# Three early steps of a two-layer float32 kernel: recurrence vector and W_out, Hadamard products in the T banks, norm factors

## The chip, the cores and the metric

The kernel runs on one core of one Trainium2 chip. The metric is the device time of one execution in microseconds (us), as a median of several runs. Engines are named as in the profile: PE is TensorE (matmuls; PEld its weight loads), DVE is VectorE, ACT is ScalarE, POOL is GpSimd, SP is SyncE, which here issues nearly all DMAs.

## What is computed

Input x is 4 x 512 x 256 in float32. Two layers, each: a layer norm, a token mixer s, a gated feed-forward g with its own three weights, and x + s * silu(g).

```
xn = layernorm(x)
# layer 0: the mixer is a recurrence whose state starts at zero, so only one step is left
xi  = xn @ W_in.T
y   = sum over states of (C_real * B_real - C_imag * B_imag) * xi      # (the theta terms multiply a zero state)
s   = xn + rmsnorm(y @ W_out.T, norm_w)
# both feed-forwards
hidden = fwht(silu(xn @ W1.T) * (xn @ W3.T)) ;  g = hidden @ W2.T       # fwht: Walsh-Hadamard over 1024
x = x + s * silu(g)
# layer 1: the mixer is causal attention with qkv, o_proj, gamma, beta, plus the residual
```

The Hadamard transform is moved from the activations to W2. The recurrence is folded into one 256 x 256 matrix M = W_in.T diag(k) W_out.T, with the vector k = sum over states of (B_real C_real - B_imag C_imag), and attention's weights into two matrices A and V.

## The kernel before

**Arithmetic.** Most products are float32 made of three TensorE passes: each operand is split into a high part (written by ACT, a copy to the type fp32r) and a low part (the difference, by DVE or POOL). `mm3` (L357 to L359) issues hi x hi, hi x lo, lo x hi. The products that make M, A and V (L425, L435, L440) are plain float32.

**Stages.** The tokens are four groups of 512 rows, and each layer passes over all four: eight groups n = 0 to 7. A group has eight chunks (0 to 7) of 128 hidden units: PE makes gate and up products into GU (`up_chunk`), ACT takes silu into `hf` (L721) and makes the high part of the last chunk's hidden (L647), DVE multiplies (L997, the `chunk` helper) and makes the low part (L841, `hid_lo_chunk`). Then PE mixes (`recurrent_mix` with M, or attention), and the next group begins with the down products of the last one (`down_chunk`, bank pair O).

**The head (group 0)** also has all preparation in it: turning and splitting W1, W3, W2, the Hadamard products and butterflies of W2 (butterflies on POOL, L1204 to L1218), and M, A, V. Every engine's order is written out by hand in its own `block0_head`. The steps around the change:

- DVE `k_vector` (L868 to L875) makes k; it waits for `small_loaded`, which nine loads raise: A_theta, B and C parts, W_in, norm_w, gamma, beta. It stands after chunk 4 and the next group's normalise (L914).
- ACT scales W_in's four parts by k (L759) after chunk 5.
- DVE `turn_wout` (L925, two transposes of `woutT`) stands after chunk 5.
- PE `small_m` (L425, 16 matmuls in the trace) stands after chunk 6 and waits for both of them; after chunk 7 comes `small_av` (L435, L440; it waits for DVE's `turn_wqkv`), then `recurrent_mix(0)`, and then PE waits for `sm_lo` at 3: DVE's low parts of M, A and V (`small_lo`).
- DVE's `w2_sums` (L857) and `w2_lo` and ACT's `w2_hi` (L688) finish W2 between chunks 6 and 7.

**The second layer's weights** are prepared in groups 1 to 3. For each of four pairs of W2 row blocks, PE makes a Hadamard product of two matmuls (`next_hadamard`, L401 and L402) into bank O[:, 1], and ACT scales it into U (`pair_u`, L670). The O bank is also what `down_chunk` writes, so groups 1 to 3 begin with a wait for `u_ready`, and `next_hadamard` waits for `gateT_ready` (ACT has read O). T's two banks are used in the head and in the attention scores and not between.

**The norm factors** of the second layer: POOL makes c2, DVE turns it into `c2T` (L976, `turn_c2`), SP stores it (L289) and spreads it to all partitions as `c2B` (L291). SP's queue is in order: in group 3 it holds the gate's transfer, then `spread_c2(0)`, then `move_rows(4)` (store `swap_rows`, L254, and four reads, L259). The rows that `move_rows` brings are scaled with c2B on DVE (L986), split on ACT (L702, L798, L647) and POOL (L1306), and PE's first attention product of group 4 (GU<-ZT,AR) needs them.

Of the kernel before, what the change touches and what calls it, by code (L numbers as in the profile page):

```python
# [22 lines left out]
ACT = mybir.ActivationFunctionType  # L23
AX_X = mybir.AxisListType.X

P = 128
# [6 lines left out]
def two_block_kernel(nc, x_in, W_in, W_out, A_theta, B_real, B_imag, C_real, C_imag, norm_w,  # L33
                     W1_0, W2_0, W3_0, qkv, o_proj, gamma, beta, W1_1, W2_1, W3_1, consts, out):
    NB, ROWS, D = x_in.shape
    H = W1_0.shape[0]
# [4 lines left out]
    MC = NM // P  # L41
    PAIRS = HC // 2
# [18 lines left out]
    with ExitStack() as ctx:  # L61
# [3 lines left out]
        def sem(name):  # L65
            return ctx.enter_context(nc.semaphore(name))
# [45 lines left out]
        with ExitStack() as early:  # L112
            win = sb("win", [P, MC, D], F32, early)
# [71 lines left out]
        c2_line = nc.dram_tensor("c2_line", [P, Q], F32).ap()  # L185
        c2_turned = sem("c2_turned")
        w_turned, wx_hi, wx_lo, natx_hi, natx_ready = sem("w_turned"), sem("wx_hi"), sem("wx_lo"), sem("natx_hi"), sem("natx_ready")
        wout_loaded, wqkv_loaded, wo_loaded = sem("wout_loaded"), sem("wqkv_loaded"), sem("wo_loaded")
        wout_turned, wqkv_turned, win_scaled = sem("wout_turned"), sem("wqkv_turned"), sem("win_scaled")
        xnext_loaded = sem("xnext_loaded")  # L190
# [34 lines left out]
        def _(sp):  # L225
# [74 lines left out]
            sp.wait_ge(w2_tr, 1)  # L300
            load_pair(0, 2, stage[:, 0, :, :], stage_loaded[0])
            for i, m in enumerate((A_theta, B_real, B_imag, C_real, C_imag)):
                sp.dma_start(ssm[:, i, :, :], m.rearrange("c (a p) s -> p (c a) s", p=P)).then_inc(small_loaded, 16)
            sp.dma_start(win[:, :, :], W_in.rearrange("(a p) k -> p a k", p=P)).then_inc(small_loaded, 16)
            load_blocks(woutT[:, :, :].rearrange("p m d -> p (m d)"), W_out, wout_loaded)
            sp.wait_ge(w2_tr, 2)
            load_pair(0, 3, stage[:, 1, :, :], stage_loaded[1])
# [39 lines left out]
                t_at = (NB - 1) * TILES  # L347
                sp.dma_start(last_part(out_dram, t_at, q), last_part(X, t_at, q)).then_inc(out_stored, 16)
            sp.wait_ge(out_stored, 16 * (NB - 1 + len(LAST_PARTS)))
        N_SMALL = 9  # L350


        @block.tensor
        def _(pe):
# [41 lines left out]

            def next_hadamard(i):

                pe.wait_ge(u_ready, i)
                pe.wait_ge(natx_ready, i - PAIRS + 1)  # L400
                pe.matmul(O[:, 1, :], hadmR[:, :], w2nat[:, 0, :, :].rearrange("p a d -> p (a d)"), start=True, stop=False)  # L401
                pe.matmul(O[:, 1, :], hadmR[:, :], w2nat[:, 1, :, :].rearrange("p a d -> p (a d)"), start=False, stop=True).then_inc(h_done, 1)  # L402

            def head_hadamard(i):
                if i == 0:
# [149 lines left out]
                pe.wait_ge(sm_lo, 3)  # L555

            def block0_group(n):
                pe.wait_ge(u_ready, PAIRS + (0, 1, 3)[n - 1])
                for i in range(HC):
                    down_chunk(0, n - 1, i)  # L560
                for c in range(HC):
                    up_chunk(0, n, c, False)
                    if c == 1 and n > 1:
                        pe.wait_ge(gateT_ready, 2 * n)
                        next_hadamard(PAIRS + 2 * n - 3)
                if n < 3:
                    pe.wait_ge(gateT_ready, 2 * n)
                    next_hadamard(PAIRS + 2 * n - 2)
                recurrent_mix(n)

# [73 lines left out]
        def _(act):  # L644
# [22 lines left out]
            def pair_u(l, i, j):  # L667

                act.wait_ge(h_done, i + 1)
                act.activation(U[l][:, 2 * j:2 * j + 2, :].rearrange("p a d -> p (a d)"), O[:, 1, :], ACT.Copy, scale=float(H) ** -0.5).then_inc(u_ready, 1)  # L670

            def nat_hi(i, nat):

                if not (isinstance(i, int) and i == 0):
                    act.wait_ge(h_done, i)
                hi(nat[:, 0, :, :].rearrange("p a d -> p (a d)"), O[:, 0, :], w2_tr, i + 1, w2nat_hi)
# [54 lines left out]
            def block0_head():  # L731
                act.dma_start(ident[:, :], consts[:, 0, :]).then_inc(ident_loaded, 16)
                flat = [R[:, 0, :, :].rearrange("p k d -> p (k d)") for R in (MR, AR, VR)]
                hi(W1T[0][:, 0, :, 0:2 * P], GU[:, 0, 0, :].rearrange("p (k h) -> p k h", k=KC), w_tr, 1, w_hi)
                first_x_hi()
                hi(W3T[0][:, 0, :, 0:2 * P], GU[:, 0, 1, :].rearrange("p (k h) -> p k h", k=KC), w_tr, 2, w_hi)
                nat_hi(0, w2nat)
                act.wait_ge(hadm_loaded, 16)
                act.activation(hadmR[:, :], hadm[:, :], ACT.Copy).then_inc(hadm_ready, 1)
                chunk(0, 0, True)  # L740
                pair_hi(0, 1, 1)
                pair_u(0, 0, 0)
                nat_hi(1, w2nat)
                chunk(0, 1, True)
                pair_u(0, 1, 1)
                pair_hi(0, 2, 2)
                nat_hi(2, w2nat)
                chunk(0, 2, True)
                chunk(0, 3, True)
                pair_u(0, 2, 2)  # L750
                pair_hi(0, 3, 3)
                nat_hi(3, w2nat)
                chunk(0, 4, True)
                chunk(0, 5, True)
                pair_u(0, 3, 3)
                hi(gb[:, :, :].rearrange("p g k -> p (g k)"), O[:, 0, 0:2 * KC], gb_tr, 1, gb_ready)
                act.wait_ge(kvec_ready, 1)
                for m in range(MC):
                    act.activation(win[:, m, :], win[:, m, :], ACT.Identity, scale=kvec[:, m:m + 1]).then_inc(win_scaled, 1)  # L759
                chunk(0, 6, True)  # L760
                hi(flat[0], O[:, 0, :], sm_mm, 1, sm_hi)
                w2_hi(0)
                chunk(0, 7, True)
                hid_hi_chunk(0, 7)
                small_hi([(flat[1], T[:, 0, :]), (flat[2], T[:, 1, :])], 2, sm_mm, 2, sm_hi)
                act.wait_ge(mask_loaded, 16)
                act.activation(identR[:, :], ident[:, :], ACT.Copy).then_inc(const_ready, 1)
                act.activation(maskR[:, :], mask[:, :], ACT.Copy).then_inc(const_ready, 1)
# [68 lines left out]
        def _(dve):  # L837
# [24 lines left out]

            def k_vector():

                dve.wait_ge(small_loaded, 16 * N_SMALL)
                flat = [ssm[:, i, :, :].rearrange("p a s -> p (a s)") for i in range(5)]
                kp = [kprod[:, i, :, :].rearrange("p a s -> p (a s)") for i in (0, 1)]
                dve.tensor_tensor(kp[0], flat[1], flat[3], ALU.mult).then_inc(kstep, 1)  # L868
# [148 lines left out]
            def between_chunks(n, c, last=False):  # L1017
# [12 lines left out]
                if c == 0 and not last:  # L1030
                    stats(n + 1, ((n + 1) % NB) * TILES)
                if c == (4 if n < NB else 3) and not last:
                    if n >= NB - 1:
                        turn_c2(n + 1)
                    dve.wait_ge(combined, 4 * n)
                    normalise(n + 1, ((n + 1) % NB) * TILES)
                if c == (5 if n < NB else 4) and not last:
                    x_turn(n + 1)
                if c == 5 and n >= NB:
                    p_lo(n - NB)  # L1040

# [27 lines left out]
            def block0_head():  # L1069
# [13 lines left out]
                pair_lo(0, 2, 2)  # L1083
                nat_lo(2, w2nat)
                chunk(0, 2)
                chunk(0, 3)
                dve.wait_ge(xnext_loaded, 16)
                pair_lo(0, 3, 3)
# [1 line left out]
                stats(1, TILES)  # L1090
                chunk(0, 4)
                normalise(1, TILES)
                k_vector()
                chunk(0, 5)
                turn_wout()
                x_turn(1)
                chunk(0, 6)
                turn_wqkv()
# [3 lines left out]
                chunk(0, 7)  # L1102
                w2_lo(0, 1)
                dve.wait_ge(xrest_loaded, 16)
                small_lo(1)
                small_lo(2)
                hid_lo_chunk(0, HC - 1)
# [245 lines left out]
```

## Time and profile before

| | us |
|---|---|
| median of 3 runs (362.18 to 363.77) | 362.24 |
| the profiled execution, its own time | 364.02 |
| its span, from first to last instruction | 362.2 |
| PE busy in the span | 353.7 (98%) |
| DVE busy | 251.1 (69%) |
| ACT busy | 167.7 (46%) |
| POOL busy | 104.2 (29%) |

The granted TensorE clock is full in all slices but one: 38 to 41.4 us is at half speed. PE's busy time counts matmuls with modelled ends, so it hides short gaps; start-to-start times of neighbouring matmuls show them better. A timeline row gives start, duration, engine, line, operation and operands, how many merged, and in brackets the idle time before it with what ended it.

### The profile page before, as it was taken

The numbers are of one execution on the slowest core, as the hardware profiler recorded it, in microseconds if no ns is written. First come the engines' busy times: TensorE is split into PE (matmuls) and PEld (weight loads), VectorE is DVE, ScalarE is ACT, GpSimd is POOL, SyncE is SP. The second block draws the span as 40 slices with busy tenths as digits, with TensorE's granted clock in tenths as the row PEclk, the third lists the DMA queues.
The fourth block names the chain that finished last, engine by engine and source line by source line (L and its number), as shares of the span: only waits on it lengthen the run. The fifth ranks groups of instructions, "written<-read, shape, count | busy, mean of one in ns | idle before, by whom it ended". The sixth has DMA issues, their size and how long they took to land.

```text
span 362.2 us, 4969 instructions
## 1 busy us (share of the span) xinstructions
PE 353.7 (98%) x1785; PEld 299.6 (83%) x1785; DVE 251.1 (69%) x482; ACT 167.7 (46%) x326; POOL 104.2 (29%) x122
## 2 busy tenths in 40 slices
PE   8998899999999999999999999999999999999996
PEld 5886788888888888887888888888888888888896
DVE  5669954896479945977568894688636887356645
ACT  2865361357135624345285544644446454454510
POOL 2165310165315953474007030060300603004000
PEclk9999899999999999999999999999999999999999
DMA  7999686305252303040142501424105342054001
GB/s 238 251 183 225 154 111 57 116 2 139 36 138 39 116 2 116 3 133 14 60 144 64 144 0 58 139 67 149 57 22 168 74 123 81 0 186 112 22 3 58
DMA packets 69648, 34.44 MB, mean 95 GB/s; under 512 B 40692, under 2 KB 69624, under 8 KB 69624
## 3 DMA queue, kind: packets, MB, share of 16 engines
q1 hardware_dynamic: 69480, 34.06, 37.0%
q8 instruction: 14, 0.23, 0.3%
q14 instruction: 10, 0.08, 0.1%
q10 hardware_dynamic: 144, 0.07, 0.1%
HBM read 21.99 MB, written 12.12 MB: 94 GB/s over the span
## 4 chain that ended last, share of the span: by engine, by line
PE 76%; DVE 12%; ACT 4%; DMA 3%; issue 2%; SPq 1%; POOL 1%; ACTq 0%; DVEq 0%
PE GU L357 14%; PE GU L359 14%; PE GU L358 14%; PE O L357 8%; PE O L358 7%; PE O L359 7%; DVE hid L841 3%; DVE hf L997 2%; DVE rows L1015 2%; PE O L425 1%; DMA stage<-in_L_ffn_W 1%; DVE rows L914 1%; DMA swap_rows<-GX 1%; PE T L357 1%; PE T L359 1%
## 5 line engine op out<-in xcount | busy, mean ns | idle before, releaser
L721 ACT ACTIVATE hf<-GU 128x512 f32<-128x512 f32 x64 | 38.2, 598 | 80.9 <-DVE hid L841 62.7
L997 DVE TENSOR_TENSOR hf<-hf,GU 128x512 f32<-128x512 f32 x64 | 43.5, 680 | 30.9 <-PE GU L359 25.0
L841 DVE TENSOR_TENSOR hid<-hf,hid 128x512 fp32r<-128x512 f32 x64 | 52.4, 820 | 0.3
L357 PE MATMUL GU<-XT,W1T 128*128 128x512 f32 x128 | 50.5, 395 | 0.0
L359 PE MATMUL GU<-XT,W1T 128*128 128x512 f32 x128 | 49.9, 390 | 0.0
L358 PE MATMUL GU<-XT,W1T 128*128 128x512 f32 x128 | 49.8, 389 | 0.0
L357 PE MATMUL GU<-XT,W3T 128*128 128x512 f32 x128 | 49.8, 389 | 0.0
L359 PE MATMUL GU<-XT,W3T 128*128 128x512 f32 x128 | 49.8, 389 | 0.0
L358 PE MATMUL GU<-XT,W3T 128*128 128x512 f32 x128 | 49.8, 389 | 0.0
L357 PE MATMUL O<-hid,W2hi 128*128 128x512 f32 x112 | 44.1, 394 | 0.7 <-ACT U L670 0.7
L358 PE MATMUL O<-hid,W2hi 128*128 128x512 f32 x112 | 43.7, 390 | 0.0
L359 PE MATMUL O<-hid,W2lo 128*128 128x512 f32 x112 | 43.7, 390 | 0.0
L647 ACT ACTIVATE hid<-hf 128x512 fp32r<-128x512 f32 x64 | 40.0, 624 | 6.2 <-DVE hf L997 6.2
L1265 POOL TENSOR_TENSOR X<-X,rows 128x256 f32<-128x256 f32 x28 | 24.3, 900 | 31.5 <-DVE rows L1015 31.5
L1223 POOL TENSOR_TENSOR vtmp<-varb,ln_eps 128x4 f32<-128x4 f32 x7 | 1.4, 201 | 98.2 <-DVE varb L909 98.2
L359 PEld LDWEIGHTS GU<-XT,W1T 128*128 128x128 f32 x128 | 24.0, 188 | 5.1
L359 PEld LDWEIGHTS GU<-XT,W3T 128*128 128x128 f32 x128 | 24.0, 188 | 5.1
L357 PEld LDWEIGHTS GU<-XT,W3T 128*128 128x128 f32 x128 | 24.0, 188 | 5.0
L358 PEld LDWEIGHTS GU<-XT,W3T 128*128 128x128 f32 x128 | 24.0, 188 | 5.0
L357 PEld LDWEIGHTS GU<-XT,W1T 128*128 128x128 f32 x128 | 24.0, 188 | 4.9 <-DVE hf L997 0.3
L358 PEld LDWEIGHTS GU<-XT,W1T 128*128 128x128 f32 x128 | 24.1, 188 | 4.6
L357 PEld LDWEIGHTS O<-hid,W2hi 128*128 128x128 f32 x112 | 21.0, 188 | 5.8 <-ACT U L670 1.1
(204 smaller groups left out, 724.4 us busy)
## 6 DMA issues: line engine op xcount, KB each, us to landing
swap_rows<-GX SPq DMA_DIRECT2D x7, 512.0 KB, 3.4
sT<-swap_rows SPq DMA_DIRECT2D x28, 128.0 KB, 2.7
swap_gate<-GX SPq DMA_DIRECT2D x7, 512.0 KB, 2.9
sT<-swap_gate SPq DMA_DIRECT2D x28, 128.0 KB, 2.8
stage<-in_L_ffn_W SPq DMA_DIRECT2D x12, 256.0 KB, 4.5
swap_p<-PX SPq DMA_DIRECT2D x4, 640.0 KB, 3.2
PL<-swap_p SPq DMA_DIRECT2D x16, 160.0 KB, 3.2
stage<-in_L_ffn_W SPq DMA_DIRECT2D x32, 64.0 KB, 2.7
```

Of the source, the lines that this page charges most:

```text
L357: pe.matmul(o, lhs(0), rhs(0), start=start, stop=False)
L358: pe.matmul(o, lhs(0), rhs(1), start=False, stop=False)
L359: return pe.matmul(o, lhs(1), rhs(0), start=False, stop=stop)
L425: last = pe.matmul(O[:, 0, k * D:(k + 1) * D], win[:, m, k * P:(k + 1) * P], woutT[:, m, :], start=(m == 0), stop=(m == MC - 1))
L647: act.activation(dst, src, ACT.Copy).then_inc(done, 1)
L721: act.activation(hf[:, c % 2, :], GU[:, c % 2, 0, :], ACT.Silu).then_inc(silu_done, 1)
L841: dve.tensor_tensor(dst, src, hi_part.bitcast(F32), ALU.subtract).then_inc(done, 1)
L914: last = dve.tensor_scalar(rows2[n % 2][:, t, :], X[:, bass.ds(x_at + t, 1), :].rearrange("p a d -> p (a d)"), mv[:, t, 0:1], rstd[:, t:t ...
L997: dve.tensor_tensor(hf[:, c % 2, :], hf[:, c % 2, :], GU[:, c % 2, 1, :], ALU.mult).then_inc(mul_done, 1)
L1015: dve.tensor_tensor(st, st, turned[:, :, t, :, :].rearrange("p j k a -> p k j a"), ALU.mult).then_inc(prod_ready, 1)
L1223: pool.tensor_tensor(vtmp[:, :], varb[:, :], ln_eps[:, :], ALU.add).then_inc(rstd_step, 1)
L1265: pool.tensor_tensor(xt, xt, rows2[n % 2][:, t, :], ALU.add).then_inc(combined, 1)
```

## The change

1. **Recurrence's vector.** The six loads of k and W_in get a semaphore of their own, `kv_loaded`; `small_loaded` keeps three. `k_vector` moves on DVE from after `normalise(1)` to after chunk 2, and ACT's scaling of W_in from after chunk 5 to before chunk 4. The order of the loads stays.
2. **W_out's turn** moves on DVE from after chunk 5 to before it.
3. **Hadamard products** of the second layer are written to T[:, i % 2] and read from there; the waits for `gateT_ready` go, the wait for `u_ready` becomes one lower, and only group 1 still begins with a wait for `u_ready`.
4. **Norm factors.** In group 3 alone, `turn_c2` moves from before `normalise` at chunk 4 to the end of chunk 3.

```diff
-                sp.dma_start(ssm[:, i, :, :], m.rearrange("c (a p) s -> p (c a) s", p=P)).then_inc(small_loaded, 16)
-            sp.dma_start(win[:, :, :], W_in.rearrange("(a p) k -> p a k", p=P)).then_inc(small_loaded, 16)
+                sp.dma_start(ssm[:, i, :, :], m.rearrange("c (a p) s -> p (c a) s", p=P)).then_inc(kv_loaded, 16)
+            sp.dma_start(win[:, :, :], W_in.rearrange("(a p) k -> p a k", p=P)).then_inc(kv_loaded, 16)
...
             def next_hadamard(i):
 
-                pe.wait_ge(u_ready, i)
+                pe.wait_ge(u_ready, i - 1)
                 pe.wait_ge(natx_ready, i - PAIRS + 1)
-                pe.matmul(O[:, 1, :], hadmR[:, :], w2nat[:, 0, :, :].rearrange("p a d -> p (a d)"), start=True, stop=False)
-                pe.matmul(O[:, 1, :], hadmR[:, :], w2nat[:, 1, :, :].rearrange("p a d -> p (a d)"), start=False, stop=True).then_inc(h_done, 1)
+                pe.matmul(T[:, i % 2, :], hadmR[:, :], w2nat[:, 0, :, :].rearrange("p a d -> p (a d)"), start=True, stop=False)
+                pe.matmul(T[:, i % 2, :], hadmR[:, :], w2nat[:, 1, :, :].rearrange("p a d -> p (a d)"), start=False, stop=True).then_inc(h_done, 1)
...
             def block0_group(n):
-                pe.wait_ge(u_ready, PAIRS + (0, 1, 3)[n - 1])
+                if n == 1:
+                    pe.wait_ge(u_ready, PAIRS)
...
                     if c == 1 and n > 1:
-                        pe.wait_ge(gateT_ready, 2 * n)
                         next_hadamard(PAIRS + 2 * n - 3)
                 if n < 3:
-                    pe.wait_ge(gateT_ready, 2 * n)
                     next_hadamard(PAIRS + 2 * n - 2)
...
-                if c == (4 if n < NB else 3) and not last:
-                    if n >= NB - 1:
+                    if n >= NB:
                         turn_c2(n + 1)
...
+                if c == 3 and n == NB - 1:
+                    turn_c2(n + 1)
```

The two moves within DVE's head are best seen in its order of instructions. From after chunk 4's second half to x's turn, before (kprod and kvec are the recurrence's vector, hf<-hf,GU is a chunk's product, hid<-hf,hid the low part of the chunk before it, GX<-rows the turn of x):

```order
L914 TENSOR_SCALAR rows<-X,mv,rstd 128x256 x4
L868 TENSOR_TENSOR kprod<-ssm 128x64
L869 TENSOR_TENSOR kprod<-ssm 128x64
L871 SCALAR_TENSOR_TENSOR kprod<-ssm,kprod 128x64
L873 TENSOR_TENSOR kprod<-kprod 128x64
L875 TENSOR_REDUCE kvec<-kprod 128x4
L997 TENSOR_TENSOR hf<-hf,GU 128x512
L841 TENSOR_TENSOR hid<-hf,hid 128x512
L925 STREAM_TRANSPOSE woutT<-woutT 128x512 x2
L954 STREAM_TRANSPOSE GX<-rows 128x4x4x32 x2
L997 TENSOR_TENSOR hf<-hf,GU 128x512
L841 TENSOR_TENSOR hid<-hf,hid 128x512
```

The same place now (all line numbers are one higher):

```order
L998 TENSOR_TENSOR hf<-hf,GU 128x512
L842 TENSOR_TENSOR hid<-hf,hid 128x512
L915 TENSOR_SCALAR rows<-X,mv,rstd 128x256 x4
L926 STREAM_TRANSPOSE woutT<-woutT 128x512 x2
L998 TENSOR_TENSOR hf<-hf,GU 128x512
L842 TENSOR_TENSOR hid<-hf,hid 128x512
L955 STREAM_TRANSPOSE GX<-rows 128x4x4x32 x2
L998 TENSOR_TENSOR hf<-hf,GU 128x512
L842 TENSOR_TENSOR hid<-hf,hid 128x512
```

And after chunk 2's two instructions (the first two rows here), where chunk 3's product stood next:

```order
L998 TENSOR_TENSOR hf<-hf,GU 128x512
L842 TENSOR_TENSOR hid<-hf,hid 128x512
L869 TENSOR_TENSOR kprod<-ssm 128x64
L870 TENSOR_TENSOR kprod<-ssm 128x64
L872 SCALAR_TENSOR_TENSOR kprod<-ssm,kprod 128x64
L874 TENSOR_TENSOR kprod<-kprod 128x64
L876 TENSOR_REDUCE kvec<-kprod 128x4
L998 TENSOR_TENSOR hf<-hf,GU 128x512
```

Between the chunk's products and x's turn the five small instructions are gone, W_out's two transposes are ahead of chunk 5 and no longer behind it, and the five stand ahead of chunk 3.

On PE, the end of group 1 and the start of group 2: the last mixing product and the first down product. Before:

```order
L357 MATMUL GU<-MR,XT 128x256
L358 MATMUL GU<-MR,XT 128x256
L359 MATMUL GU<-MR,XT 128x256
L357 MATMUL O<-hid,W2hi 128x512 [waits w2_ready,hid_ready,u_ready]
L358 MATMUL O<-hid,W2hi 128x512
L359 MATMUL O<-hid,W2lo 128x512
```

Now:

```order
L358 MATMUL GU<-MR,XT 128x256
L359 MATMUL GU<-MR,XT 128x256
L360 MATMUL GU<-MR,XT 128x256
L358 MATMUL O<-hid,W2hi 128x512 [waits w2_ready,hid_ready]
L359 MATMUL O<-hid,W2hi 128x512
L360 MATMUL O<-hid,W2lo 128x512
```

The wait for `u_ready` at the first down product is gone. On DVE in group 3, from chunk 2's product to x's turn, before:

```order
L997 TENSOR_TENSOR hf<-hf,GU 128x512
L841 TENSOR_TENSOR hid<-hf,hid 128x512
L997 TENSOR_TENSOR hf<-hf,GU 128x512
L841 TENSOR_TENSOR hid<-hf,hid 128x512
L976 STREAM_TRANSPOSE c2T<-c 128x32
L914 TENSOR_SCALAR rows<-X,mv,rstd 128x256 x4
L997 TENSOR_TENSOR hf<-hf,GU 128x512
L841 TENSOR_TENSOR hid<-hf,hid 128x512
L954 STREAM_TRANSPOSE GX<-rows 128x4x4x32 x2
```

Now:

```order
L998 TENSOR_TENSOR hf<-hf,GU 128x512
L842 TENSOR_TENSOR hid<-hf,hid 128x512
L977 STREAM_TRANSPOSE c2T<-c 128x32
L998 TENSOR_TENSOR hf<-hf,GU 128x512
L842 TENSOR_TENSOR hid<-hf,hid 128x512
L915 TENSOR_SCALAR rows<-X,mv,rstd 128x256 x4
L998 TENSOR_TENSOR hf<-hf,GU 128x512
L842 TENSOR_TENSOR hid<-hf,hid 128x512
L955 STREAM_TRANSPOSE GX<-rows 128x4x4x32 x2
```

The turn of the norm factors (c2T<-c) stands one chunk earlier.

## Rows read from the trace of the kernel before

**Rows 1.** PE's waits: engine, tile, line, what ended them; total, times, longest (us)

```profile
PE O L425 <- issue: 2.4, 1, 2.4
PE O L357 <- ACT U L670: 0.7, 2, 0.4
```

**Rows 2.** Timeline, PE in the head

```profile
37.23 5.38 PE L425 MATMUL O<-woutT,win 128*128 128x256 f32 x16 [2.40 <-issue]
...
45.18 1.89 PE L435 MATMUL T<-wqkvT 128*128 128x256 f32 x8
...
51.51 0.39 PE L357 MATMUL O<-hid,W2hi 128*128 128x512 f32 x1
```

**Rows 3.** Stretch: sum; busy of PE, PEld, DVE, ACT, POOL; granted clock; DMA share; GB/s

```profile
38.00:39.00 1.00, 1.00 (x4) 0.82 (x3) 1.00 (x3) 0.00 (x0) 1.00 (x1) 0.50 0.62 96
```

**Rows 4.** Timeline, DVE in the head

```profile
24.13 0.69 DVE L997 TENSOR_TENSOR hf<-hf,GU 128x512 f32<-128x512 f32 x1 [1.43 <-PE GU L359]
...
32.23 0.22 DVE L868 TENSOR_TENSOR kprod<-ssm 128x64 f32<-128x64 f32 x1
...
33.57 0.68 DVE L997 TENSOR_TENSOR hf<-hf,GU 128x512 f32<-128x512 f32 x1
34.16 1.75 DVE L841 TENSOR_TENSOR hid<-hf,hid 128x512 fp32r<-128x512 f32 x1
35.84 1.29 DVE L925 STREAM_TRANSPOSE woutT<-woutT 128x512 f32<-128x512 f32 x2
37.06 1.25 DVE L954 STREAM_TRANSPOSE GX<-rows 128x512 f32<-128x512 f32 x2
...
38.81 1.21 DVE L841 TENSOR_TENSOR hid<-hf,hid 128x512 fp32r<-128x512 f32 x1
39.95 1.88 DVE L925 STREAM_TRANSPOSE wqkvT<-wqkvT 128x512 f32<-128x512 f32 x3
...
49.46 0.69 DVE L841 TENSOR_TENSOR VR<-T,VR 128x512 fp32r<-128x512 f32 x1 [0.79 <-ACT VR L647]
```

**Rows 5.** Timeline, POOL in the head

```profile
34.08 1.28 POOL L1211 TENSOR_TENSOR U<-U 128x512 f32<-128x512 f32 x1
...
37.12 2.36 POOL L1218 TENSOR_TENSOR U<-U 128x1024 f32<-128x1024 f32 x1
```

**Rows 6.** Timeline, ACT in the head

```profile
33.69 1.71 ACT L759 ACTIVATE win<-win,kvec 128x256 f32<-128x256 f32 x4 [1.21 <-DVE kvec L875]
```

**Rows 7.** Timeline of SP's queue: W_out's four loads

```profile
14.54 3.78 SPq L242 DMA_DIRECT2D woutT<-in_L_attn_W_out  x4
```

**Rows 8.** The tile woutT: landing time of its four loads after issue

```profile
DMA to landing us min/median/max: 4.5/5.0/5.2
```

**Rows 9.** Timeline, PE from group 1 to group 2

```profile
87.38 0.28 PE L359 MATMUL GU<-MR,XT 128*128 128x256 f32 x1
88.01 0.50 PE L357 MATMUL O<-hid,W2hi 128*128 128x512 f32 x1 [0.35 <-ACT U L670]
```

**Rows 10.** Timeline from group 3 to group 4: DVE, SP's queue, ACT, PE

```profile
151.83 0.20 DVE L976 STREAM_TRANSPOSE c2T<-c 128x32 f32<-128x32 f32 x1
...
154.14 0.38 SPq L291 DMA_DIRECT2D c2B<-c_line  x1
155.91 0.36 SPq L254 DMA_DIRECT2D swap_rows<-GX  x1
...
164.61 1.16 ACT L702 ACTIVATE XT<-sT 128x512 fp32r<-128x512 f32 x2 [1.03 <-DMA sT<-swap_rows]
...
169.92 0.50 PE L357 MATMUL GU<-ZT,AR 128*128 128x512 f32 x1 [0.43 <-POOL ZT L1306]
```

**Rows 11.** The chain of waits, in order of time, at the same place

```profile
155.91 4.47 DMA swap_rows<-GX
```

**Rows 12.** The tile swap_rows: landing time of its stores and reads

```profile
DMA to landing us min/median/max: 2.3/2.8/4.5
```

**Rows 13.** The tile c2B: landing time of its four loads

```profile
DMA to landing us min/median/max: 4.8/4.9/5.0
```

More of the change, by code:

```diff
@@ L187, in two_block_kernel @@
         w_turned, wx_hi, wx_lo, natx_hi, natx_ready = sem("w_turned"), sem("wx_hi"), sem("wx_lo"), sem("natx_hi"), sem("natx_ready")
+        kv_loaded = sem("kv_loaded")
         wout_loaded, wqkv_loaded, wo_loaded = sem("wout_loaded"), sem("wqkv_loaded"), sem("wo_loaded")
@@ L349, in _ @@
             sp.wait_ge(out_stored, 16 * (NB - 1 + len(LAST_PARTS)))
-        N_SMALL = 9
+        N_KV, N_SMALL = 6, 3
         @block.tensor
@@ L669, in pair_u @@
                 act.wait_ge(h_done, i + 1)
-                act.activation(U[l][:, 2 * j:2 * j + 2, :].rearrange("p a d -> p (a d)"), O[:, 1, :], ACT.Copy, scale=float(H) ** -0.5).then_inc(u_ready, 1)
+                bank = O[:, 1, :] if l == 0 else T[:, i % 2, :]
+                act.activation(U[l][:, 2 * j:2 * j + 2, :].rearrange("p a d -> p (a d)"), bank, ACT.Copy, scale=float(H) ** -0.5).then_inc(u_ready, 1)
             def nat_hi(i, nat):
@@ L752, in block0_head @@
                 nat_hi(3, w2nat)
+                act.wait_ge(kvec_ready, 1)
+                for m in range(MC):
+                    act.activation(win[:, m, :], win[:, m, :], ACT.Identity, scale=kvec[:, m:m + 1]).then_inc(win_scaled, 1)
                 chunk(0, 4, True)
@@ L756, in block0_head @@
                 hi(gb[:, :, :].rearrange("p g k -> p (g k)"), O[:, 0, 0:2 * KC], gb_tr, 1, gb_ready)
-                act.wait_ge(kvec_ready, 1)
-                for m in range(MC):
-                    act.activation(win[:, m, :], win[:, m, :], ACT.Identity, scale=kvec[:, m:m + 1]).then_inc(win_scaled, 1)
                 chunk(0, 6, True)
@@ L863, in k_vector @@
             def k_vector():
-                dve.wait_ge(small_loaded, 16 * N_SMALL)
+                dve.wait_ge(kv_loaded, 16 * N_KV)
                 flat = [ssm[:, i, :, :].rearrange("p a s -> p (a s)") for i in range(5)]
@@ L1085, in block0_head @@
                 chunk(0, 2)
+                k_vector()
                 chunk(0, 3)
@@ L1092, in block0_head @@
                 normalise(1, TILES)
-                k_vector()
+                turn_wout()
                 chunk(0, 5)
-                turn_wout()
                 x_turn(1)
@@ L1104, in block0_head @@
                 dve.wait_ge(xrest_loaded, 16)
+                dve.wait_ge(small_loaded, 16 * N_SMALL)
                 small_lo(1)
```

## Prediction

> **What bounds the kernel now.** TensorE does. I read the list of PE's waits first [rows 1]: outside the start it waits at three kinds of place only, and each is one that the change aims at, so the question is not whether PE's waits are the bound but how much of each wait is left when its present cause is gone. The first is 2.40 us ahead of `small_m`, marked "issue" because several semaphores end it. The timelines tell which [rows 2, 4, 6]: ACT ends the scaling of W_in at 33.69 + 1.71 = 35.40, DVE ends the turn of W_out at 35.84 + 1.29 = 37.13, and PE starts at 37.23. So W_out's turn is last and the scaled W_in stands only 1.7 us ahead of it; both must move for the wait to go. The wait has a second price. `small_m` takes 5.38 us for 16 matmuls, while eight of the same shape take 1.89 [rows 2]; two such eights would take 3.8, so it runs 1.6 us longer. The stretches say why: a little after PE's idle time the granted clock is 0.50, the 1.2 GHz level [rows 3]. The second kind are two waits on ACT's U at the start of groups 2 and 3, 0.7 us in all [rows 1, 9]. The third is 0.43 us on POOL's ZT at the start of group 4 [rows 10].
>
> **Part 1 and 2: the head.** *The vector.* Its five DVE instructions take 33.57 - 32.23 = 1.34 us [rows 4] and go into a slot in which DVE idled 1.43 us for PE, ahead of chunk 3's product at 24.13. So they cost nothing there, if their six loads have landed by about 22.7. The trace doesn't show W_in's landing. It was issued just ahead of W_out's four loads, of which the first began to issue at 14.54 and each landed 4.5 to 5.2 us after issue [rows 7, 8]; taken as the nearest row this gives about 19.7 for W_in, 3 us early. From the other side it had landed by 32.23, where the vector was made without a wait for it. I take 19.7 and keep 32.23 for a rival. *Scaling W_in*, 1.71 us on ACT [rows 6], now stands before chunk 4's silu, which becomes about 1 us later; DVE multiplies that chunk only after the next group's statistics, so it doesn't notice. Cost nothing. *W_out's turn*, 1.29 us, takes exactly the place that the vector leaves, and ends at about 33.45. `small_m` then has all inputs when chunk 6 is done, at 37.23 - 2.40 = 34.83.
>
> So far PE would gain 2.40 + 1.6 = 4.0 us. The question is who is late next. PE would reach `small_av` at about 41 (before: 45.18) and the end of the mixing at about 47.5 (before: 51.51). What it needs there is DVE's: first the turned qkv, then `sm_lo` at 3, the low part of V. DVE was full from 30.9 to 42.9, and the moves take 1.3 us out of that stretch. Do its later steps come 1.3 us earlier? The rows say mostly not. A low part `hid<-hf,hid` reads two SBUF tensors and takes about 0.7 us when POOL is quiet, but 1.75 at 34.16, where POOL's butterfly had begun at 34.08, and 1.21 at 38.81, inside POOL's 37.12 to 39.48 [rows 4, 5]: each ends some 0.5 us after a POOL instruction does. The transposes at 35.84 and 37.06 run at full rate beside the same POOL work. With W_out's turn gone from behind it, x's turn comes at 35.8, chunk 6's product at 37.0, and the low part after it asks at 37.6, where POOL's long butterfly has just begun. It waits until 39.4 and ends at 39.9, as before. The turn of qkv is then at 39.9, as before [rows 4], and the 1.3 us are lost to a wait. Everything behind it on DVE (w2_sums, the parts of W2, chunk 7) keeps its time but for 0.1 to 0.2 us, and of the row at 49.46 only the 0.79 us of waiting for ACT's V goes, since PE makes V earlier now. So V's low part is ready at 49.46 + 0.69 - 0.79 - 0.15 = 49.2, PE starts the down products there, and **the head gains 51.51 - 49.2 = 2.3 us**. Two short idle times of about 0.8 us are new on PE, ahead of `small_av` (41.0 to 41.8) and ahead of the down products (48.3 to 49.2).
>
> The upper bound is 4.0, all of PE's loss. It is reached if the low part that asked at 34.16 gets in ahead of POOL. This is close: it now asks at 32.23 + (37.06 - 35.84) + 0.59 = 34.04, and POOL asks at 34.08, or at 34.00 if its first butterfly is no longer slowed by the small products of the vector. The lower bound is 0.6: both new idle times bring the slow clock, at up to 1.6 each less what the wait for DVE hides; the nearest rows are 2.40 us of idle time, which brought it, and 0.43, which didn't.
>
> The Trainium skill says in "SBUF — State Buffer", section "Who interferes with whom", that a DVE instruction with two SBUF inputs and a GpSimd one contend for a shared port pair, held for a whole instruction by whichever issues first, and that a DVE instruction with one SBUF input doesn't contend. The trace agrees with it: 1.75 against 0.7 us, and the transposes undisturbed. It speaks against this change: if the engines shared evenly and nothing waited, the head would give its 4.0 us; by the rule it gives 2.3.
>
> **Part 3: the Hadamard products.** No instruction is added. From the last mixing product to the first down product PE takes 88.01 - 87.38 = 0.63 us where mixing products follow each other at 0.12, and the first one back takes 0.1 longer for its weights; so 0.6 us at each of two places [rows 9], though the wait list has 0.35 [rows 1]. With U's copy out of T, the next thing to be late would be chunk 7's low part, which the third down chunk needs 2.7 us later; it ends at 87.6. So **1.2 us**. Bounds 0.7 (the waits as listed) and 1.3. The dropped waits for gateT_ready ended nothing in the list of waits: 0. Nobody else uses T in these groups.
>
> **Part 4: the norm factors.** DVE's c2T comes at about 149.9 and not 151.83; its 0.20 us fall into an idle time ahead of chunk 4. c2B then is issued at about 152.1 instead of 154.14 [rows 10]. The store of the rows is still issued at about 155.8, since DVE's turn of x sets that. In the trace it took 4.47 us to land where the median of this tile is 2.8 [rows 11, 12], and c2B, 4.9 us to land [rows 13], was under way for 3.1 us of it. With 1.2 us left of that overlap I take 1.0 us earlier for the rows; bounds 0 (overlap isn't the cause) and 1.7. ACT has idled 1.03 us for them [rows 10], so at most that passes on. PE's wait of 0.43 with the refill behind it, 0.7 by start-to-start times as in part 3, needs 0.6 us. So **0.7 us**, bounds 0 and 0.7.
>
> **Sum.** 2.3 + 1.2 + 0.7 = 4.2 us. Everything behind group 4 is bound by PE without a wait, so it shifts whole. The profiled execution's 364.02 us, 1.8 outside its span, would be 359.8; the median of the runs is 362.24, 1.8 less, and I carry the difference over: **358.0 us**.
>
> **Rivals.** (A) *DVE wins the tie at 34.04.* Then chunk 4's low part is done at 34.7, POOL is set back 0.6 us, the turn of qkv comes at 37.7 and V's low part at about 47.1, before PE asks. No wait of PE is left in the head: 4.0 + 1.2 + 0.7 = 5.9, time 356.3. For it: 0.04 us on one side; against: POOL's first butterfly is probably 0.08 earlier too, and at 0.08 us POOL won in this trace. (B) *A smaller sum*: one new idle time brings the slow clock (1.6), or part 4 gives nothing (0.7) together with part 3's lower bound (0.5). Times 359.6 and 359.2; both new idle times slow, 361. (C) *Slower.* DVE takes its steps in order, so if the six loads land late, the wait for kv_loaded holds chunk 3's product, and with it PE's chunk 5, which starts at 28.4 and needs that product. With a landing at L, PE loses L + 0.9 + 0.7 - 28.4. It eats the 4.2 us from L = 31.0 on; at 32.2, the latest that the trace allows, it is 5.4 us lost, 363.4. Against it are the loads behind these ones, landed by 23. (D) *It doesn't do what it says*: another input ends `small_m`'s wait at about 37 and only parts 3 and 4 are left, 360.3.
>
> **Chances.** Forecast 0.58, A 0.25, B 0.10, C 0.02, D 0.05. A measurement of this kernel can tell 0.5%, 1.8 us, from no change: faster is below 360.4. The forecast, A, most of B and half of D lie there, 0.93; I say 0.92. Within it 0.06, slower 0.02. The range takes in A, with 0.4 for its own error, and B's single slow clock: 355.9 to 359.8, leaving out C, D and the worst of B.
>
> **What the profile after would show.** Head: no idle time ahead of `small_m`, which takes 3.6 us at full clock; PE idle ahead of L436 and of the first down product at the head's end, 0.8 each; DVE's low part after chunk 6 long, some 2.3 us, and qkv's turn at 39.9 (in rival A at 37.7, and the idle times gone). At the starts of groups 2 and 3 no wait on U. In group 3 swap_rows landing in about 3.4 us and no wait on ZT. I am wrong if DVE waits for kv_loaded at 22.7, if the low part behind chunk 5 is 0.7 us long, or if PE's clock falls at a new idle time.

## The result, and the profile after

The changed kernel takes 357.88 us (median of 5 runs, 357.71 to 358.28). The kernel before, run beside it, takes 362.18 us (5 runs). The ratio is 0.987, with a 95% interval of 0.9848 to 0.9893, so the change gains 4.3 us. The prediction was 358.0. The number held, but the head did not go as forecast: two errors there nearly cancel, and most of what follows is about how they do.

PE's waits in the changed kernel, all of them (engine, tile, line, what ended them; total, times, longest, in us). In the rows of after, PE's and most of DVE's lines stand one number higher than in [rows 1 to 10], POOL's four higher:

```profile
PE GU L526 <- DVE hf L1073: 1.5, 1, 1.5
PE GU L365 <- DMA stage<-in_L_ffn_W: 0.4, 1, 0.4
PE GU L365 <- DVE rows L899: 0.3, 1, 0.3
```

All three lie in the first 9 us. Every wait of [rows 1, 10] is gone. The table of engines can't show this: PE is at 98% of a span of 356.1 us, as it was before:

```profile
PE   350.6 (98%) x1785; PEld 297.9 (84%) x1785; DVE 248.8 (70%) x482; ACT 167.5 (47%) x326; POOL 105.2 (30%) x122
```

The head after, as timelines: DVE, then POOL, then PE.

```profile
32.17 1.30 DVE L926 STREAM_TRANSPOSE woutT<-woutT 128x512 f32<-128x512 f32 x2
33.40 0.65 DVE L998 TENSOR_TENSOR hf<-hf,GU 128x512 f32<-128x512 f32 x1
33.97 0.69 DVE L842 TENSOR_TENSOR hid<-hf,hid 128x512 fp32r<-128x512 f32 x1
...
36.37 1.21 DVE L842 TENSOR_TENSOR hid<-hf,hid 128x512 fp32r<-128x512 f32 x1
37.51 1.88 DVE L926 STREAM_TRANSPOSE wqkvT<-wqkvT 128x512 f32<-128x512 f32 x3
```

```profile
34.19 1.61 POOL L1215 TENSOR_TENSOR U<-U 128x512 f32<-128x512 f32 x1
```

```profile
34.68 0.39 PE L360 MATMUL GU<-XT,W3T 128*128 128x512 f32 x1
34.90 3.61 PE L426 MATMUL O<-woutT,win 128*128 128x256 f32 x16
...
47.42 0.39 PE L358 MATMUL O<-hid,W2hi 128*128 128x512 f32 x1
```

Chunk 4's low part asks at 33.97, POOL's butterfly at 34.19 (an engine asks where its row starts). The low part takes 0.69 us and the butterfly 1.61. In [rows 4, 5] it was the other way round, 1.75 and 1.28. This is rival A. The turn of qkv is at 37.51 and not at 39.95, `small_m` follows chunk 6 without idle time in 3.61 us, and the first down product is at 47.42 and not at 51.51, 4.09 us earlier (rival A: 4.0, forecast: 2.3). Chunk 6's last matmul starts 0.24 us later than in [rows 2] (34.68 against 34.44), so from that matmul on the gain is 4.33 us. It is 0.3 more than rival A's 4.0: `small_m` takes 3.61 us where the prediction put two eights of 1.89, and the step to it from chunk 6's last matmul is 2.57 us shorter (2.79 to 0.22), where the list of waits had 2.40.

The step from group 1 to group 2, PE; it answers [rows 9]:

```profile
83.29 0.28 PE L360 MATMUL GU<-MR,XT 128*128 128x256 f32 x1
83.41 0.40 PE L358 MATMUL O<-hid,W2hi 128*128 128x512 f32 x1
```

Start to start it is 0.12 us where it was 0.63. And group 3 to group 4, SP's queue and PE; it answers [rows 10]:

```profile
146.10 0.38 SPq L292 DMA_DIRECT2D c2B<-c_line  x1
150.43 0.36 SPq L255 DMA_DIRECT2D swap_rows<-GX  x1
153.87 1.27 SPq L260 DMA_DIRECT2D sT<-swap_rows  x3
```

```profile
163.71 0.40 PE L360 MATMUL O<-hid,W2lo 128*128 128x512 f32 x1
163.94 0.39 PE L358 MATMUL GU<-ZT,AR 128*128 128x512 f32 x1
```

The reads of the rows follow the store by 153.87 - 150.43 = 3.44 us, where the store took 4.47 to land [rows 11], and PE enters group 4 without a wait.

One number does not fit a simple account. From execution to execution, rival A's gain is 4.0 + 1.2 + 0.7 = 5.9 us, and between the two profiled executions it is 364.02 - 357.93 = 6.1. Between the medians it is 4.3. So the profiled execution of before is not like the median one, and the first experiment had to show how they differ.

### The profile page after: what moved, and what is told of

It is laid out like the page before. It is cut to its first block, busy times and chain, and to the rows that moved or that the text cites. A ratio compares the mean times of both kernels' runs of the same rounds, so it can differ in the third digit from the quotient of the medians.

```text
span 356.1 us, 4969 instructions
## 1 busy us (share of the span) xinstructions
PE 350.6 (98%) x1785; PEld 297.9 (84%) x1785; DVE 248.8 (70%) x482; ACT 167.5 (47%) x326; POOL 105.2 (30%) x122
## 2 busy tenths in 40 slices
DMA packets 69648, 34.44 MB, mean 97 GB/s; under 512 B 40692, under 2 KB 69624, under 8 KB 69624
## 4 chain that ended last, share of the span: by engine, by line
PE 96%; DVE 2%; DMA 1%; POOL 0%; issue 0%; ACT 0%
PE GU L358 20%; PE GU L360 20%; PE GU L359 20%; PE O L358 8%; PE O L359 8%; PE O L360 8%; PE O L426 1%; PE T L358 1%; DMA X<-in_L_attn_x 1%; PE T L360 1%; PE T L359 1%; PE O L509 1%; PE O L508 1%; PE O L507 1%; PE T L365 1%; PE O L365 1%
## 5 line engine op out<-in xcount | busy, mean ns | idle before, releaser
L842 DVE TENSOR_TENSOR hid<-hf,hid 128x512 fp32r<-128x512 f32 x64 | 51.2, 801 | 0.3
L1310 POOL TENSOR_TENSOR ZT<-zfull,ZT 128x512 fp32r<-128x512 f32 x8 | 11.3, 1415 | 47.5 <-ACT ZT L647 47.2
```

The source lines that it names most:

```text
L842: dve.tensor_tensor(dst, src, hi_part.bitcast(F32), ALU.subtract).then_inc(done, 1)
L1310: pool.tensor_tensor(zT[1][k], zfull[:, k, :], zT[0][k].bitcast(F32), ALU.subtract).then_inc(zt_ready, 1)
```

## The experiments

The kernels before and after ran beside these. Before stood at 362.1 to 362.23 us in each comparison, so a kernel's gain is read from its median. The 95% interval of a gain reaches 0.5 to 1 us to either side.

**The kernel before once more.**

> The kernel before, unchanged, to see clock and span of each of its runs. Theory 1 (the slow clock in the head of the profiled execution is an accident of single executions): most runs take about 362.2 us with a granted clock of 1.00 and a span of about 360.4, and the few near 363.8 have 0.995 and 362.2; the profile may show small_m in 3.6 us in place of 5.4. Theory 2, the forecast's own (the clock falls in every execution, since the 2.40 us of idle time are in every one): all runs have 0.995, and the 1.6 us between the runs come from somewhere else.

Measured: 362.29 us, ratio 0.9999 (0.9976 to 1.0022). The executions of this one program come in two groups. Of 83 runs of it, 19 stand at 363.62 to 364.45 us with a mean granted clock of 0.994 or 0.995, the other 64 at 361.55 to 363.22 with at least 0.998. I call the smaller group the slow kind. The profile of before that the prediction rests on (364.02 us, clock 0.995) is of the slow kind. The one taken here, with a span of 360.3 us, is of the other. Its head, DVE, POOL and PE:

```profile
33.22 0.22 DVE L873 TENSOR_TENSOR kprod<-kprod 128x64 f32<-128x64 f32 x1
...
34.21 1.08 DVE L841 TENSOR_TENSOR hid<-hf,hid 128x512 fp32r<-128x512 f32 x1
35.21 1.29 DVE L925 STREAM_TRANSPOSE woutT<-woutT 128x512 f32<-128x512 f32 x2
```

```profile
33.30 0.73 POOL L1204 TENSOR_TENSOR U<-U 128x256 f32<-128x256 f32 x1 [1.94 <-ACT U L670]
...
34.82 1.61 POOL L1211 TENSOR_TENSOR U<-U 128x512 f32<-128x512 f32 x1
```

```profile
26.00 0.52 PE L364 MATMUL O<-ident,stage 128*128 128x128 f32 x3 [0.45 <-DMA stage<-in_L_ffn_W]
...
35.30 0.39 PE L359 MATMUL GU<-XT,W3T 128*128 128x512 f32 x1
36.60 1.75 PE L425 MATMUL O<-woutT,win 128*128 128x256 f32 x7 [0.91 <-issue]
...
49.78 0.50 PE L357 MATMUL O<-hid,W2hi 128*128 128x512 f32 x1 [0.38 <-DVE VR L841]
```

Here DVE is first twice: the vector's fourth product (L873) asks at 33.22, ahead of POOL's 33.30, and the low part is far ahead of the long butterfly (34.21 against 34.82); its 1.08 us are those of a low part that asks inside POOL's row before it, 34.00 to 34.74. The idle time is 0.91 us, not 2.40, and the clock stays at the 2.4 GHz level. In the profile of the prediction these two rows of before show the lost first meeting:

```profile
32.75 0.65 DVE L873 TENSOR_TENSOR kprod<-kprod 128x64 f32<-128x64 f32 x1
```

```profile
32.49 0.82 POOL L1204 TENSOR_TENSOR U<-U 128x256 f32<-128x256 f32 x1 [1.60 <-ACT U L670]
```

L873 takes 0.43 us longer, so the low part asks late, loses the second meeting and takes 1.1 us longer itself. What goes with the order is a load of weights: PE waits 0.45 us for it at 26.00, and POOL's butterflies, which need PE's product through ACT, come that much later while DVE comes later by less. Measured against the start of chunk 6's last matmul, POOL's first butterfly is 1.95 to 2.00 us ahead in all seven profiles of kernels that have the vector in its old place. L873 is 2.07 or 2.08 ahead where PE had waited for this load (three profiles, waits of 0.31 to 0.45, L873 0.22 us long), and 1.69 to 1.89 where it had not (four profiles, 0.65 to 0.70 long). By start-to-start times of PE's rows (0.87 us from T<-ident,stage to O<-ident,stage where nothing waits) the four had been delayed by 0 to 0.18 us and the three by 0.47 to 0.61. So in all seven the order of the two went with this load. Between the two profiles of the kernel before the difference is 1.9 us (364.02 against 362.13). That the load decides is read from these profiles; no run set its landing.

**Parts 1 and 2 alone.**

```
 chunk(0, 2)
+k_vector()
 chunk(0, 3)
 ...
-k_vector()
+turn_wout()
 chunk(0, 5)
-turn_wout()
```

> The kernel before with parts 1 and 2 alone (recurrence's vector and W_out's turn moved). Theory 1: DVE's low part behind chunk 5 gets in ahead of POOL as in the profile after, no wait of PE is left in the head, and against typical runs the gain is the idle time alone, 2.4 us: 359.8. Theory 2 (the forecast): two idle times of 0.8 us on PE ahead of the attention's weights and of the first down product, and 2.3 us gained: 359.9. The times are alike; the profile tells them apart. Were the slow clock in all runs of before and no wait left, the gain would be 4.0: 358.2.

Measured: 359.85 us, ratio 0.9922 (0.9895 to 0.9949), 2.4 us gained. Behind the first 10 us no wait of PE is left in the head, and the low part (34.16) is ahead of POOL (34.27) by 0.11 us. One of the 8 runs stands apart, at 362.17 us with a clock of 0.998, 2.3 us above the median. It has no profile, and what happened in it stays open.

**Part 1 alone** (the vector moved, W_out's turn where it was).

> The kernel before with part 1 alone (the vector and W_in's scaling early, W_out's turn still behind chunk 5). Theory: W_out's turn is the last input of small_m; with the vector's 1.3 us gone from ahead of it, it ends about 35.3, PE idles some 0.5 us ahead of small_m and little or nothing later: 360.2, 2.0 us below before. Rival (each part is half of the gain and neither works alone): 361.5 or more.

Measured: 360.43 us, ratio 0.9934 (0.9913 to 0.9956), 1.8 us gained. In the profiled execution `small_m` has no idle time ahead of it, where 0.5 us was expected:

```profile
33.78 1.30 DVE L926 STREAM_TRANSPOSE woutT<-woutT 128x512 f32<-128x512 f32 x2
```

```profile
35.40 3.61 PE L426 MATMUL O<-woutT,win 128*128 128x256 f32 x16
```

W_out's turn ends at 35.08, just ahead of `small_m`. But here PE had waited 0.63 us for its load at 25.9 us, so it came late. In parts 1 to 3 below, where PE did not wait, `small_m` starts at 34.53, and a turn that ends at 35.08 would hold it by some 0.5 us. So the profile doesn't show that part 2 is idle; the medians of part 1 and of parts 1 and 2 are 0.6 us apart.

**Part 2 alone** (W_out's turn ahead of chunk 5, the vector where it was).

> The kernel before with part 2 alone (W_out's turn ahead of chunk 5, the vector where it was). Theory: now W_in's scaling is last, at 35.4, PE idles 0.6 us ahead of small_m; DVE reaches chunk 5 1.2 us later than before and chunk 6's steps at the same time as before, so it idles again at the head's end for V's low part, 0.4 to 0.8: 361.0. Rival (a port tie decides, not the inputs): as before, 362.2, with the slow clock in some runs.

Measured: 361.57 us, ratio 0.9977 (0.9963 to 0.9992), 0.7 us gained where 1.2 was expected. The wait changes its cause and the second one doubles. PE's rows:

```profile
35.44 3.72 PE L425 MATMUL O<-woutT,win 128*128 128x256 f32 x16 [0.56 <-ACT win L759]
49.06 0.50 PE L357 MATMUL O<-hid,W2hi 128*128 128x512 f32 x1 [0.75 <-DVE VR L841]
```

No run of its 12 has a mean clock below 0.998: L873 is held (0.65 us), but W_out's turn no longer stands behind the low part. From chunk 6's last matmul to the first down product it takes 14.57 us, as in the kernel before (14.48), so its 0.7 us are not gained in that stretch.

**Part 3 alone** (the Hadamard products in T).

> The kernel before with part 3 alone (Hadamard products in T). Both theories: two waits of 0.6 us by start-to-start times go, 1.2 us: 361.0. Rival: only what the list of waits has, 0.7 us: 361.5; or another input is late at the same place and nothing is gained: 362.2.

Measured: 361.14 us, ratio 0.9961 (0.994 to 0.9983), 1.1 us gained; PE's waits on U are gone. 4 of its 12 runs are of the slow kind, the profiled one among them (idle 2.27 us), and it shows the clock behind the idle time. The stretches (columns as in [rows 3]):

```profile
38.00:39.00 1.00, 1.00 (x4) 0.83 (x3) 1.00 (x3) 0.00 (x0) 1.00 (x1) 0.58 0.61 96
39.00:40.00 1.00, 1.00 (x4) 0.77 (x3) 1.00 (x2) 0.00 (x0) 0.93 (x1) 0.50 0.66 154
```

**Part 4 alone** (the norm factors at chunk 3).

> The kernel before with part 4 alone (norm factors turned at chunk 3). Forecast: 0.7 us, 361.5, with the rows' store landing in 3.4 us in place of 4.5 and no wait of PE on ZT. Rival: the store is slow for another reason than the spread of the norm factors, lands in 4.5 us again, and nothing is gained: 362.2.

Measured: 361.64 us, ratio 0.9981 (0.9959 to 1.0003), 0.6 us gained, an interval that touches nothing gained. In its trace c2B is issued at 149.32, the store at 153.64, and the reads follow at 157.10, 3.46 us later, without a wait on ZT. In the kernel before of the same comparison these are 152.44, 154.21 and 158.66, 4.45 us.

**Parts 1 to 3** (without part 4).

> The kernel before with parts 1, 2 and 3, part 4 left out. Theory (the parts add): 358.5, 0.6 more than after, with the rows' store landing in 4.3 to 4.5 us and a wait on ZT of 0.3 to 0.5. Rival (with PE earlier by part 3, or DVE by parts 1 and 2, the wait on ZT changes size): 0 or over 1 us.

Measured: 358.5 us, ratio 0.9884 (0.986 to 0.9909), 0.6 us more than the full change. So part 4's 0.6 is found from both sides. The wait on ZT is back with 0.4 us, and the store takes 4.38 us again. In this profile chunk 4's low part and POOL's long butterfly ask almost together, and DVE is not held:

```profile
33.89 0.67 DVE L842 TENSOR_TENSOR hid<-hf,hid 128x512 fp32r<-128x512 f32 x1
```

```profile
33.87 1.83 POOL L1213 TENSOR_TENSOR U<-U 128x512 f32<-128x512 f32 x1
```

**The meeting of DVE and POOL, first attempt.**

```
 turn_wout()
+for _ in range(3):
+    dve.memset(kprod[:, 1, 0, _:_ + 1], 0.0)
 chunk(0, 5)
```

> The kernel after with three DVE writes of one element each into spare memory behind W_out's turn, so that DVE's low part behind chunk 5 asks some 0.4 us later, after POOL's butterfly has begun. Theory (the forecast's mechanism is real, it was only the tie that fell the other way): the low part takes 1.6 us in place of 0.7, DVE's chain is late for PE at the head's end, two idle times of together 1.2 to 1.8 us appear, 359.3 (258 ns more on POOL's side don't matter). Rival (the port plays no part for the time): only DVE's own 0.4 us less its slack of 0.35, 357.9 to 358.0.

Measured: 358.35 us, ratio 0.9883 (0.9859 to 0.9907). This settles nothing. The three memsets ran side by side with a product that was under way, so the low part was not set back against POOL (34.44 against 34.72) and took 0.74 us.

```profile
33.84 0.68 DVE L998 TENSOR_TENSOR hf<-hf,GU 128x512 f32<-128x512 f32 x1
33.85 0.07 DVE L1099 MEMSET kprod<- 128x1 f32 x3
34.44 0.74 DVE L842 TENSOR_TENSOR hid<-hf,hid 128x512 fp32r<-128x512 f32 x1
```

**Second attempt: a delay of 0.48 us ahead of the low part.**

```
 turn_wout()
+dve.memset(c2B[:, :], 0.0)
 chunk(0, 5)
```

> The changed kernel with one extra DVE instruction, a memset of c2B (128x512, no SBUF input, the tile is unused until group 3) between the turn of W_out and chunk 5's part of the head; nothing is left out of the computation. It should take some 0.3 to 0.6 us, so chunk 4's low part asks at about 34.4 us instead of 33.97, after POOL's first butterfly (34.2). Theory 'order of asking': POOL is first, the low part takes about 1.7 us instead of 0.69, DVE is late behind it, its next low part waits for POOL's long butterfly, and PE waits ahead of the down products or of L436: 1.2 to 2 us lost, about 359.5. Rival 'order is irrelevant, DVE gets in anyway': only the 0.45 us delay on an engine with slack, 357.9 to 358.1.

Measured: 360.06 us (359.75 to 360.34), ratio 0.9937 (0.9914 to 0.996). DVE, POOL and PE:

```profile
34.78 1.65 DVE L842 TENSOR_TENSOR hid<-hf,hid 128x512 fp32r<-128x512 f32 x1
...
38.15 2.43 DVE L842 TENSOR_TENSOR hid<-hf,hid 128x512 fp32r<-128x512 f32 x1
40.49 0.70 DVE L926 STREAM_TRANSPOSE wqkvT<-wqkvT 128x512 f32<-128x512 f32 x1
```

```profile
34.60 1.28 POOL L1216 TENSOR_TENSOR U<-U 128x512 f32<-128x512 f32 x1
```

```profile
35.08 0.39 PE L360 MATMUL GU<-XT,W3T 128*128 128x512 f32 x1
35.31 3.61 PE L426 MATMUL O<-woutT,win 128*128 128x256 f32 x16
...
42.43 1.99 PE L436 MATMUL T<-wqkvT 128*128 128x256 f32 x8 [0.78 <-DVE wqkvT L926]
...
49.72 0.51 PE L358 MATMUL O<-hid,W2hi 128*128 128x512 f32 x1 [0.71 <-DVE VR L842]
```

**The same delay behind the low part.**

```
 chunk(0, 5)
+dve.memset(c2B[:, :], 0.0)
 x_turn(1)
```

> The changed kernel with the same memset one step later, behind chunk 4's low part and ahead of the turn of x. DVE loses the same time, but the low part still asks ahead of POOL. Theory 'order of asking': low part 0.7 us, POOL set back as in the changed kernel, the rest of DVE's steps have slack: 357.9 to 358.1. Rival 'any delay on DVE costs': the same time as the kernel with the memset one step earlier.

Measured: 358.02 us (357.78 to 358.66), ratio 0.988 (0.9855 to 0.9905), the time of the changed kernel. The low part, ahead of POOL's 34.90:

```profile
34.57 0.80 DVE L842 TENSOR_TENSOR hid<-hf,hid 128x512 fp32r<-128x512 f32 x1
35.42 0.48 DVE L1099 MEMSET c2B<- 128x512 f32 x1
```

One and the same instruction costs 2.0 us more in one place than a step later, where it costs 0.1 to 0.2 against the changed kernel. All six runs of the one lie above all six of the other. What differs in the profiles is who asks first: the low part takes 1.65 us in the one and 0.80 in the other, the next low part 2.43 and 0.72, and both waits of PE end on DVE.

**The same two delays in the kernel before.** The memset stands between the vector and `chunk(0, 5)` in the first, between `chunk(0, 5)` and `turn_wout()` in the second.

> The kernel before with the same memset between the vector and chunk 5's part, so that chunk 4's low part asks some 0.3 us or more after POOL's first butterfly in every execution. Theory 'order of asking decides between the two kinds of executions': nearly all runs are of the kind that is rare in the kernel before: granted clock 0.994 to 0.995, 363.6 to 364.6 us, with over 2.4 us of idle time ahead of small_m and 5.4 us for it. Rival 'the kinds have another cause': most runs keep clock 1.00 and stand at 362.2 to 362.8, the memset's own length later.

Measured: 362.42 us, ratio 1.001 (0.9992 to 1.0029), and only 3 of 12 runs of the slow kind. The expectation missed. In the profiled execution PE had waited 0.40 us for the load, L873 was ahead of POOL, and the low part asked at 34.37, still 0.12 ahead:

```profile
34.37 0.68 DVE L841 TENSOR_TENSOR hid<-hf,hid 128x512 fp32r<-128x512 f32 x1
```

The margin at the low part had been 34.82 - 34.21 = 0.61 us, more than this delay. The profiles say that the kind is decided earlier, at L873, which the memset does not touch.

> The kernel before with the same memset behind chunk 4's low part, ahead of the turn of W_out. The turn, and with it small_m, comes the memset's length later (about 0.45 us), but the order in which DVE and POOL ask is that of the kernel before. Theory 'order of asking': idle ahead of small_m about 1.35 us in most executions, clock 1.00, median about 362.6, the rare kind as often as before or so. Rival 'what matters is only how late W_out's turn is': the same as with the memset one step earlier.

Measured: 362.83 us, ratio 1.0024 (1.0003 to 1.0045): 4 of 12 runs at 364.2 to 364.6 us with the clock at 0.994 or 0.995. The profiled one is among them, with 2.76 us of idle time ahead of `small_m` and 5.31 us for it. With 12 runs this can't be told from the 19 of 83 of the kernel before, as expected. The idle time of the common kind was not seen, and its median, 362.75 us, is 0.15 above the one expected.

## Why the prediction was right, and where it was not

**Part 1's costs at nothing held.** DVE's rows of after answer to the first of [rows 4]: the vector's first product follows the work ahead of it without a wait for the loads, and chunk 3's product has 0.51 us of idle time left ahead of it.

```profile
22.56 0.22 DVE L869 TENSOR_TENSOR kprod<-ssm 128x64 f32<-128x64 f32 x1
...
24.07 0.69 DVE L998 TENSOR_TENSOR hf<-hf,GU 128x512 f32<-128x512 f32 x1 [0.51 <-PE GU L360]
```

Rival C fell with this, and rival D with `small_m`'s missing wait.

**The head: the wrong branch, and a term that was right for it.** The forecast let POOL win the meeting at 34.04 and took 2.3 us; it called for two idle times of 0.8 us, a low part of about 2.3 us behind chunk 6 and qkv's turn near 39.9. None of it is in the profile after. All of it is in the kernel that makes DVE ask late: 0.78 and 0.71 us of idle time, a low part of 2.43 us, qkv's turn at 40.49 (in an execution that is 0.64 us behind that of [rows 2] at chunk 6). From chunk 6's last matmul to the first down product that kernel takes 14.64 us against 17.07 in the profile of before, 2.4 us less. So the working of the branch was sound, and neither new idle time brought the slow clock, as the forecast chose and rival B did not. The step that failed is the choice of the branch, and the prediction's own sign of it is there: the low part behind chunk 5 is 0.69 us long. The asking times were nearly right. DVE asked at 33.97 (forecast 34.04), POOL at 34.19 (forecast 34.08, or 34.00 for an undisturbed first butterfly). POOL's 0.11 to 0.19 us come from PE's load of weights. PE's rows at it, before and after:

```profile
24.32 1.03 PE L364 MATMUL T<-ident,stage 128*128 128x128 f32 x8
25.19 0.60 PE L364 MATMUL O<-ident,stage 128*128 128x128 f32 x4
```

```profile
24.26 1.03 PE L365 MATMUL T<-ident,stage 128*128 128x128 f32 x8
25.41 0.63 PE L365 MATMUL O<-ident,stage 128*128 128x128 f32 x4
```

It is 1.15 us from one to the other after and 0.87 before. PE and POOL behind it come 0.28 us later, DVE does not. The lead of DVE grows with this delay: -0.02 us in the profile of parts 1 to 3 (no delay), 0.11 in that of parts 1 and 2 (0.15), 0.22 in the changed kernel (0.28). The first of these is the forecast's own case, a tie. There DVE still took 0.67 us, though POOL's row starts 0.02 us earlier, and in part 1 alone, where POOL's row starts 0.01 us earlier (33.17 against 33.18), it took 0.69. POOL held it with a lead of 0.07 us (34.53 against 34.60, part 3 alone), and in part 2 alone its second butterfly did with 0.03 (35.32 against 35.35). So the side on which this meeting falls turns on some 0.02 us, which the working could not give: by it POOL asked 0.04 us after DVE or 0.04 before, by the rows of the undelayed execution 0.02 before. Why 0.02 us falls to DVE no run shows; a row's start may not be the moment of asking. With DVE first the stretch takes 12.74 us, 4.3 less than the profile of before.

**The base: a difference carried over that should not have been.** The sum was made against the profiled execution (364.02) and shifted by 1.8 us to the median (362.24), as if the 1.8 were spread over the kernel. They are the slow kind's own stall, in the very place that the change works on. The other kind has 14.48 us in the stretch, so the change takes 14.48 - 12.74 = 1.7 us from it there. The base credits 17.07 - 14.48 = 2.6 us to executions that never had that stall, and the branch misses 14.64 - 12.74 = 1.9. The two nearly cancel (2.4 - 2.6 + 1.9 = 1.7), and that is why a forecast with a wrong head gave the right time. It is luck: neither error was known, and each alone would have put the forecast off by 1.6 to 1.9 us. Rival A, put on the same base, gave 356.3 and missed by 1.6.

**What makes 1.7 into 2.4.** The medians of the parts add up: 2.4 + 1.1 + 0.6 = 4.1 of 4.3. But of the head's 2.4, 0.7 are not in the stretch. About 0.2 is the slow kind's share in the median of before: without it the kernel before stands at 362.04 us in that comparison, and parts 1 and 2 gain 2.2. (Without it the parts give 2.2 + 1.0 + 0.5 = 3.7 of 4.2, so the sum is good to half a microsecond only.) The other 0.5 is ahead of the stretch. In the profiles of the kernel before (362.13 us) and of parts 1 and 2 (359.85), each close to its median, PE reaches chunk 6's last matmul at 35.30 and at 34.75, 0.55 us apart; the stretch gives 14.48 - 12.75 = 1.73, together 2.28 of 2.28. Of the 0.55, 0.46 is the load of weights, by which PE was delayed 0.61 us in the one and 0.15 in the other. A reason is at hand: in the kernel before, an execution in which PE isn't delayed falls into the slow kind, so those that are left had been. In the changed kernel the early executions keep their lead. Part 2 alone fits it: it has the stretch as before (14.57 us) and no slow kind, its profile is an early one, and PE is at chunk 6's last matmul at 34.49. This is argued from one profile a kernel, not shown.

**Part 3**: 1.2 forecast, 1.1 measured alone. **Part 4**: 0.7 forecast, 0.6 measured alone and 0.6 when taken away; c2B out of the store's way gave 1.0 us in the landing, as taken, though the experiments move the overlap only and don't tell bandwidth from order in the queues. The overlap shrank more than forecast: with the store 4.33 us behind c2B and 4.9 us for c2B to land, some 0.6 us is left of it and not 1.2.

**The slow kind is gone.** In the seven kernels that have the vector in its new place, none of 43 runs has a clock of 0.994 or 0.995. The first meeting, at L873, no longer exists there; and in the kernel that loses the second, W_out has been turned already and no long idle time follows. It does not follow that the second is never lost: the one run of parts 1 and 2 at 362.17 us is 2.3 us above its median, about what a lost meeting costs (2.0), and has no profile.

**Who asks first.** The traces show the low part at 0.69 us and POOL at 1.61 when DVE asks 0.22 us ahead, and 1.65 and 1.28 when it asks 0.18 us behind. The Trainium skill says in "SBUF — State Buffer", section "Who interferes with whom", that issue order decides which of the two engines blocks at the shared port pair, and that the pair is an exclusive lock; the traces agree with it, in both directions.

## What to carry to other kernels

Before a sum is made against a profiled execution, compare its time and its mean clock with those of the other runs; if it is apart from the median, find out in which place, since a change to that place gains a different amount in each kind. Where two engines take turns at something that one holds for a whole instruction, work out both orders and measure the asking times from a common event; then ask what moves one of them and not the other. Here it was a load of weights, which delayed PE and POOL by 0 to 0.95 us in the fourteen profiles and DVE by less (not at all where it was 0.28, by 0.6 where it was 0.95). Place the work so that the order has a margin larger than that. The changed kernel doesn't have one: with the load in time its meeting is a tie. A delay of half a microsecond on an engine with slack can cost next to nothing or 2 us, and one probe on each side of the meeting tells which.

## What the runs showed of the hardware

Of the two profiles of the kernel before, the one in which PE had not waited for a load of weights was 1.9 us slower than the one in which it had waited 0.45 us, by way of two lost meetings and the clock. In the kernel before and those with one of its parts or a memset, the granted clock fell to the 1.2 GHz level behind idle times of 2.27 to 2.76 us and stayed at 2.4 GHz behind those of 0.56 to 1.00. A low part on DVE (two inputs in SBUF) took 0.67 us in a tie with a POOL butterfly (0.02 us behind it), and 1.65 to 1.76 us when it asked 0.07 to 0.18 us behind one; it then ended 0.54 to 0.56 us behind POOL's row. Three memsets of one column each, 0.07 us in all, ran side by side with a DVE product of 0.68 us and did not set back the low part behind it.
